# The 3x3 convolution of a two-layer kernel rewritten as minimal filtering F(2,3) along the width

## What is computed

```
xn  = groupnorm(x)                                   # 32 groups of 16 channels
f   = relu(Wc @ xn + bc)                             # 512 -> 128 channels
dyn = relu(Wck . stack(gate_kernel, band_maxima) + bck)   # per image: a 3x3 kernel, 128 x 128 channels
y   = conv3x3(f, dyn) + b_ad                         # 128 -> 128 channels
x1  = x + Wf @ y + bf                                # 128 -> 512 channels
out = x1 + grouped_conv3x3(groupnorm(x1), K)         # 32 groups, 16 -> 16 channels
```

## Time and profile before

| | us |
|---|---|
| median of 3 runs | 3616.2 (3615.72 to 3616.76) |
| the profiled execution's own time | 3616.31 |
| its span from first to last instruction | 3614.6 |
| PE busy | 3498.8 (97%) |
| DVE busy | 2532.3 (70%) |
| ACT busy | 2109.9 (58%) |
| POOL busy | 965.3 (27%) |

### The profile page before, as it was taken

How to read it: one execution, slowest core, us unless ns; L and a number is a source line. 1 busy time by engine, 2 the same in 40 slices (tenths; PEclk the granted TensorE clock), 3 DMA queues, 4 the chain that set the end, 5 groups by cost and what they waited for, 6 DMA issues and landing times.

```text
span 3614.6 us, 60228 instructions
## 1 busy us (share of the span) xinstructions
PE 3498.8 (97%) x18688; PEld 2789.1 (77%) x18688; DVE 2532.3 (70%) x5365; ACT 2109.9 (58%) x3559; POOL 965.3 (27%) x1039
## 2 busy tenths in 40 slices
PE   5799999999999999999999999999999999999996
PEld 4677877777877778877778777778777778777785
DVE  7676777776767677777667777767777777776742
ACT  4365555665555665655655556655556655556654
POOL 2033222232222232222332222322222322223323
PEclk9899999999999999999999999999999999999998
DMA  5467767677767667767677667677676777676666
GB/s 122 142 193 190 190 178 185 200 195 192 185 180 195 191 184 193 190 183 197 189 188 190 186 178 207 197 190 186 178 191 194 188 195 186 182 199 187 170 156 158
DMA packets 317577, 666.88 MB, mean 184 GB/s; under 512 B 58863, under 2 KB 288242, under 8 KB 288645
## 3 DMA queue, kind: packets, MB, share of 16 engines
q1 hardware_dynamic: 317317, 663.34, 68.5%
HBM read 355.00 MB, written 308.28 MB: 184 GB/s over the span
## 4 chain that ended last, share of the span: by engine, by line
PE 90%; issue 5%; DVE 4%; DMA 1%; POOL 0%; DVEq 0%; ACT 0%; SPq 0%; POOLq 0%; ACTq 0%
PE pb L853 15%; PE pb L855 15%; PE pb L854 15%; PE pac L853 7%; PE pd L853 7%; PE pd L855 7%; PE pd L854 7%; PE pac L854 6%; PE pac L855 6%; PE pac L925 2%; PE pac L862 1%; DVE x1b L764 1%; PE ps L918 1%; DMA big<-x 0%; DVE va L596 0%
## 5 line engine op out<-in xcount | busy, mean ns | idle before, releaser
L407 POOL TENSOR_TENSOR hl<-un,hl 128x384 f16<-128x384 f32 x1024 | 937.6, 916 | 2570.2 <-ACT hl L432 2566.6
L432 ACT ACTIVATE hl<-un 128x384 f16<-128x384 f32 x1024 | 539.0, 526 | 427.8 <-PE pb L855 361.7
L428 ACT ACTIVATE un<-big,b_t,s_t 128x384 f32<-128x384 f32 x1024 | 709.7, 693 | 16.1 <-DMA big<-x_rows 16.1
L853 PE MATMUL pb<-fh,dynh 128*128 128x480 f32 (+1 forms) x1440 | 548.2, 381 | 0.0
L855 PE MATMUL pb<-fh,dynl 128*128 128x480 f32 (+1 forms) x1440 | 545.3, 379 | 0.0
L854 PE MATMUL pb<-fl,dynh 128*128 128x480 f32 (+1 forms) x1440 | 544.4, 378 | 0.0
L774 DVE SCALAR_TENSOR_TENSOR big<-pd,kout,big 96x768 f32<-96x768 f32 x256 | 258.8, 1011 | 382.6 <-PE pd L855 382.6
L853 PE MATMUL pd<-hl,k_h 128*96 128x384 f16 x1536 | 507.0, 330 | 18.8 <-POOL hl L407 18.8
L774 DVE SCALAR_TENSOR_TENSOR big<-pb,kout,big 96x768 f32<-96x768 f32 x256 | 258.9, 1011 | 351.8 <-PE pb L855 351.8
L853 PE MATMUL pb<-hl,k_h 128*96 128x384 f16 x1536 | 504.9, 329 | 0.0
L854 PE MATMUL pd<-hl,k_h 128*96 128x384 f16 x1536 | 504.8, 329 | 0.0
(11 more groups left out here) (115 smaller groups left out, 5241.6 us busy)
## 6 DMA issues: line engine op xcount, KB each, us to landing
big<-x SPq DMA_DIRECT2D x128, 1152.0 KB, 9.8
x_rows<-x1b SPq DMA_DIRECT2D x128, 1152.0 KB, 5.6
big<-x_rows SPq DMA_DIRECT2D x128, 1152.0 KB, 12.7
out<-big SPq DMA_DIRECT2D x128, 1152.0 KB, 6.2
big<-x_rows SPq DMA_DIRECT2D x256, 192.0 KB, 13.2
x_rows<-mrow SPq DMA_DIRECT2D x64, 96.0 KB, 1.9
big<-kt SPq DMA_DIRECT2D x4, 288.0 KB, 9.7
big<-kt SPq DMA_DIRECT2D x2, 192.0 KB, 11.0
```

Source lines behind the costliest of these rows:

```text
L407: pool.tensor_tensor(hl[:, g % HL_RING, 1, :, 1:W + 1], un[:, g % U_RING], hl[:, g % HL_RING, 0, :, 1:W + 1], ALU.subtract).then_inc(hl_lo, 1)
L428: act.activation(un[:, g % U_RING], t_slot(g // GQ)[:, g % GQ], ACT.Identity, bias=b_t[:, g:g + 1], scale=s_t[:, g:g + 1]).then_inc(u_done, 1)
L432: act.activation(hl[:, g % HL_RING, 0, :, 1:W + 1], un[:, g % U_RING], ACT.Copy).then_inc(hl_hi, 1)
L853: pe.matmul(acc, high_w, high_x, start=start, stop=False)
```

## The change

F(2,3) computes two neighbouring output columns of a row of a 3-tap filter with four products in place of six. From f, four planes are made ("frequencies" in the code): with columns f0..f3 of a pair these are f2 - f0 and f3 - f1 (one instruction for both), f2 + f1, and f2 - f1. The filter gets four combinations of its three taps per row: the two outer taps as they are, and (outer sum + middle) and (outer sum - middle). Four products are added over the three rows, and the two outputs are combined from them.

What is new, by engine:

- PE: the B stage has 3 tiles of 16 rows x 24 column pairs = 384 columns, 4 frequencies x 3 rows x 3 matmuls: 108 matmuls, 24 of them 360 columns wide at the image's edge. It uses 7 PSUM banks in turn.
- POOL: `v_sums` makes the four planes in three instructions a tile behind one that zeroes the border columns; `v_low` the low part of tiles 0 and 1; `y_low` that of two of the three output tiles; `dyn_sums` the tap combinations.
- ACT: `f_relu` writes f without splitting it, `v_high` the high part of the four planes (960 or 768 elements a partition), `m2_out` one product out of PSUM, `y_high` on 768 elements; `dyn_relu` and `dyn_high` take the place of one instruction.
- DVE: no `f_low`; `v_low` for tiles 2 to 4, `y_sums` and `y_rest` (four instructions of 384 elements a tile), one `y_low`. `dyn_low` moves to the start of a step. Moments and maxima of chunks 2, 3 and 0 stand in the C and D stage, those of chunk 1 alone in B.
- SP: the weights `wc` and `dyn_rows` are loaded anew for each image behind the B stage, since their place in SBUF is shared with a plane. x1's chunk and the squares also lie in planes.

The diff's core:

```diff
-EARLY = {3: (0, 1), 4: (2, 3)}
+EARLY = {1: (0, 1), 2: (2, 3)}
+WROWS = 16
+NW = H // WROWS
+WM = W // 2
+WN = WROWS * WM
+FREQ = 4
+FREQ_ORDER = (2, 3, 0, 1)
+B_BANK = [0, 1, 2, 3, 4, 5, 6, 0, 2, 3, 4, 5]
+PER_B = NW * FREQ
+POOL_TILES = 2
+POOL_Y = 2
...
-STATS_IN_B = (1, 2, 3)
...
-MOMENTS_AT = {3: (0, 0), 4: (0, 1)}
-MAXIMA_AT = {5: 0}
+GATES_AFTER = 29
+MOMENTS_AT = {0: (2, 0), 1: (2, 1), 2: (3, 0), 3: (3, 1), 4: (0, 0), 5: (0, 1)}
+MAXIMA_AT = {7: 2, 9: 3, 10: 0}
...
-KERNEL_INPUTS_AFTER = 11
-KERNELS_AFTER = 12
+CENTRED_AT = 11
+KERNEL_INPUTS_AFTER = 12
+KERNELS_AFTER = 13
...
+            def v_sums(n, t):
+                nr = TILES[t][1]
+                f, v = f_tile(t), v_tile(vl_sums, t)
+                if t == 0:
+                    reached(pool, sq_done, n * Q)
+                some = ones[:, 0:2 * nr].rearrange("p (r two) -> p r two", two=2)
+                pool.tensor_tensor(f[:, :, 0:W + 2:W + 1], some, some, ALU.subtract).then_inc(pad_done, 1)
+                pool.wait_ge(pad_done, n * NT + t + 1)
+                pool.wait_ge(f_done, n * NT + t + 1)
+                if t == 0:
+                    pool.wait_ge(dyn_done, n + 1)
+                pool.tensor_tensor(v[:, :, 0:2, :].rearrange("p r k m -> p r m k"), f[:, :, 2:W + 2].rearrange("p r (m k) -> p r m k", k=2),
+                                   f[:, :, 0:W].rearrange("p r (m k) -> p r m k", k=2), ALU.subtract)
+                even, odd = (f[:, :, 1 + i:1 + i + W - 1:2] for i in range(2))
+                pool.tensor_tensor(v[:, :, 2, :], odd, even, ALU.add)
+                pool.tensor_tensor(v[:, :, 3, :], odd, even, ALU.subtract).then_inc(v_done, 1)
...
+            def v_low(n, t):
+                pool.wait_ge(v_hi, n * NT + t + 1)
+                pool.tensor_tensor(v_tile(vl, t), v_tile(vl_sums, t), f32(v_tile(vh, t)), ALU.subtract).then_inc(v_lo_pool, 1)
...
+                for t in range(NT):
+                    v_sums(n, t)
+                    if 1 <= t <= POOL_TILES:
+                        v_low(n, t - 1)
+                for t in range(POOL_Y):
+                    y_low(n, t)
+                    if d:
+                        d_groups(n - 1, EARLY[t + 1])
                 if d:
-                    d_groups(n - 1, range(G))
-
+                    d_groups(n - 1, range(EARLY_GROUPS, G))
+                else:
+                    kernels_low()
+                if more:
+                    dyn_sums(n + 1)
...
-                act.activation(fh[:, r0 + 1:r0 + 1 + nr, 1:W + 1], pac[:, t % 2, 0:nr * W].rearrange("p (r w) -> p r w", w=W),
-                               ACT.Relu).then_inc(f_hi, 1)
+                if t == 0:
+                    reached(act, sq_done, n * Q)
+                if t == NT - 1:
+                    reached(act, hl_lo, (n - 1) * G)
+                elif t >= 2:
+                    act.wait_ge(v_done, n * NT + t - 1)
+                act.activation(f_tile(t)[:, :, 1:W + 1], pac[:, t % 2, 0:nr * W].rearrange("p (r w) -> p r w", w=W),
+                               ACT.Relu).then_inc(f_done, 1)
...
+            def v_high(n, t):
+                act.wait_ge(v_done, n * NT + t + 1)
+                if t == 0:
+                    reached(act, x1_out[Q - 1], n * 16)
+                act.activation(v_tile(vh, t), v_tile(vl_sums, t), ACT.Copy).then_inc(v_hi, 1)
...
+            def m2_out(n, t):
+                act.wait_ge(b_mm, n * PER_B + t * FREQ + 2)
+                act.activation(y_columns(t, 1), b_bank(t * FREQ + 1), ACT.Identity, bias=badc[:, 0:1],
+                               scale=0.5).then_inc(m2_done, 1)
...
+            def dyn_relu(n):
+                act.wait_ge(dyn_mm, n + 1)
+                act.activation(dynl_sums[:, :, 0:2, :], dyn_acc[:, :, 0:2 * CM].rearrange("p d (k m) -> p d k m", k=2), ACT.Relu)
+                act.activation(middle, dyn_acc[:, :, 2 * CM:3 * CM], ACT.Relu).then_inc(dyn_f, 1)
+
             def dyn_high(n):
-                act.wait_ge(dyn_mm, n + 1)
-                act.activation(dynh_banks, dyn_acc, ACT.Relu).then_inc(dyn_hi, 1)
+                act.wait_ge(dyn_g, n + 1)
+                act.activation(dynh[:, :, :, :], dynl_sums[:, :, :, :], ACT.Copy).then_inc(dyn_hi, 1)
...
-                        f_high(n, t - 1)
-                f_high(n, NT - 1)
-                for t in range(NT):
-                    if t in EARLY and d:
+                        f_relu(n, t - 1)
+                    if 2 <= t < NT:
+                        v_high(n, t - 2)
+                f_relu(n, NT - 1)
+                if d:
+                    root_second(n - 1)
+                v_high(n, NT - 2)
+                m2_out(n, 0)
+                v_high(n, NT - 1)
+                if not d:
+                    kernels(0)
+                y_high(n, 0)
+                for t in range(1, NW):
+                    if d:
                         d_groups(n - 1, EARLY[t])
+                    m2_out(n, t)
+                    if not d:
+                        kernels(t)
                     y_high(n, t)
...
+                if more:
+                    dyn_relu(n + 1)
                 square(n, Q - 1)
+                if more:
+                    dyn_high(n + 1)
...
+            def v_low(n, t):
+                vec.wait_ge(v_hi, n * NT + t + 1)
+                vec.tensor_tensor(v_tile(vl, t), v_tile(vl_sums, t), f32(v_tile(vh, t)), ALU.subtract).then_inc(v_lo_dve, 1)
...
+            def y_sums(n, t):
+
+                vec.wait_ge(m2_done, n * NW + t + 1)
+                vec.scalar_tensor_tensor(out=y_columns(t, 0), in0=b_bank(t * FREQ), scalar=0.5, in1=y_columns(t, 1),
+                                         op0=ALU.mult, op1=ALU.add)
+                vec.scalar_tensor_tensor(out=y_columns(t, 1), in0=b_bank(t * FREQ), scalar=0.5, in1=y_columns(t, 1),
+                                         op0=ALU.mult, op1=ALU.subtract).then_inc(eo_done, 1)
+
+            def y_rest(n, t):
+
+                vec.wait_ge(eo_done, n * NW + t + 1)
+                vec.wait_ge(b_mm, n * PER_B + t * FREQ + 3)
+                vec.scalar_tensor_tensor(out=y_columns(t, 0), in0=b_bank(t * FREQ + 2), scalar=-1.0, in1=y_columns(t, 0),
+                                         op0=ALU.mult, op1=ALU.add)
+                vec.wait_ge(b_mm, n * PER_B + t * FREQ + 4)
+                vec.scalar_tensor_tensor(out=y_columns(t, 1), in0=b_bank(t * FREQ + 3), scalar=badc[:, 1:2], in1=y_columns(t, 1),
+                                         op0=ALU.add, op1=ALU.add).then_inc(y_done, 1)
...
-                for t in range(NT):
-                    for i in range(t * Q, (t + 1) * Q):
-                        if i >= AHEAD:
-                            x_low(n, odd, i)
-                    if t:
-                        f_low(n, t - 1)
-                f_low(n, NT - 1)
+                if d:
+                    x1_mean_rows(n - 1)
+                dyn_low(n)
+                for i in range(AHEAD, UNITS):
+                    x_low(n, odd, i)
                 if d:
                     x1_group_means(n - 1)
                     x1_variances(n - 1)
-                y_low(n, 0)
-                for t in range(1, NT):
-                    if t == SCALES_BEFORE and d:
-                        for i in range(SCALE_STEPS):
-                            x1_scales(n - 1, i)
-                    if more and t <= len(STATS_IN_B):
-                        moments(n + 1, 1 - odd, STATS_IN_B[t - 1])
-                        maxima(n + 1, 1 - odd, STATS_IN_B[t - 1])
-                    y_low(n, t)
+                v_low(n, 2)
+                v_low(n, 3)
+                y_sums(n, 0)
+                if d:
+                    for i in range(SCALE_STEPS):
+                        x1_scales(n - 1, i)
+                v_low(n, 4)
+                y_rest(n, 0)
+                if more:
+                    moments(n + 1, 1 - odd, 1)
+                y_sums(n, 1)
+                y_rest(n, 1)
+                if more:
+                    maxima(n + 1, 1 - odd, 1)
+                y_sums(n, 2)
+                y_rest(n, 2)
+                y_low(n, 2)
...
+                r0 = t * WROWS
+                if t == 0:
+                    pe.wait_ge(v_lo_pool, POOL_TILES * (n + 1))
+                else:
+                    pe.wait_ge(v_lo_dve, (NT - POOL_TILES) * n + t + 1)
+                for j, k in enumerate(FREQ_ORDER):
+                    i = t * FREQ + j
+                    if i == 2:
+                        pe.wait_ge(f_done, (n + 1) * NT)
+                    if i == 7 or i == 10:
+                        pe.wait_ge(eo_done, n * NW + (1 if i == 7 else 2))
+                    if i == 8:
+                        pe.wait_ge(y_done, n * NW + 1)
+                    acc = b_bank(i).rearrange("p (r m) -> p r m", m=WM)
+                    for dy in (1, 0, 2):
+                        lo, hi = max(r0 + dy - 1, 0), min(r0 + dy - 1 + WROWS, H)
+                        at = lo - (r0 + dy - 1)
```

(16 more changed lines are left out.)

229 lines of the change are left out of this document (132 added, 97 removed).

## The result

The changed kernel takes **3874.2 us** (median of 4 runs, 3873.1 to 3880.3) beside 3616.1 for the kernel before: ratio 1.072, 95% interval 1.0707 to 1.0733. It is slower by 258 us. First its page, engines and the chain that ended last; in the earlier trace rows PE had 90% of the chain.

A forecast was written before the change was run, and what follows sets the result against it. PE was taken as the bound, busy nearly all of a 109.5 us step. Terms -9.9 + 9.5 + 2.9 + 2.3 + 0.5 + 3.0 gave +8.3 a step, hence 3875 us; its own range 3770 to 4020, stated range 3650 to 4010.

The forecast's parts named there:

- Products of B: B stage: 108 matmuls starting 0.184 us apart take 19.6 us in place of 29.46, -9.9 us a step.
- A, +9.5: A stage: late start, POOL and DVE taking turns, and last matmuls make 23.4 us against 13.9, +9.5 a step.
- fixed sum of turns, whoever goes first: In A, B cannot start before DVE's 15 x_low (7.7) and POOL's sums and v_low (11.4) are through, 19.1 us.
- Point (2): Sign in A: x_low mean over 1.2 us, POOL busy nearly throughout, PE waiting for xs, A 21 to 27 us.
- Root, +2.9: In B, the second tile waits for v_low 3, behind v_high 3 and root_second on ACT: +2.9 us a step, bounds 2.4 to 3.5.
- point (3): Sign in B: PE waits some 3 us for vl by DVE once behind each x1_spread.
- Way into C: C's first unit waits for the last tile's y_low, with layer 1 groups late: +2.3 us a step, bounds 0.5 to 3.5.
- Pair 8: C and D: maxima at pair 7 make the first residual behind pair 8 late, so PE waits +0.5 us.
- pair 11, +3.0: C and D: DVE's maxima and prep work after output 9 make PE wait +3.0 us more for unit 18's bank.
- point (6): Sign for PE throughout: the granted clock stays at 1.00.
- The rival: PE's clock falls in A and at B's start, 2.6 us for each of 32 steps, about 3960 us; chance 0.13.
- The third rival: A's feeding keeps PE's pace, A grows under 1.2 us, step -1.2, about 3575 us and faster; chance 0.12.

The follow-up runs named there:

- the run with one SBUF input: Changed kernel with x_low of units 5 to 19 (from image 1 on) taking its first input from PSUM instead of x, its value then wrong: 3684.1 us.
- The same kind of POOL work without consumers: The kernel before, with POOL given 36 subtractions of constant SBUF tensors in A, needed only by ACT's first layer 1 group, which waits for their end: 3701.3 us.
- the run with copies: The kernel before with nine pieces of unneeded POOL work in A, three of each piece's four instructions being one-input copies, the small first a subtraction: 3616.3 us, ratio 1.0005.

## Why the prediction was right, and where it was so by luck

Predicted 3875, measured 3874.2; 8.3 a step predicted, 8.5 measured in the mean of two steps (8.35 over 30). The terms:

- *Products of B, -9.9.* 18.8 us once nothing waits in it, hence -10.7: 0.8 off. The pace is 0.174, not 0.184. The old kernel's last tile did run at 0.182 in all its 27 matmuls of 384 columns (from the row below to D's first at 1174.23 in the earlier trace rows), so the reading was right; why the planes' matmuls are a little faster is not shown by any run.

```profile
1169.32 0.34 PE L853 MATMUL pb<-fh,dynh 128*128 128x384 f32 x1
```

- *A, +9.5.* Measured +9.0 and +8.1, mean +8.6 (+8.5 over 30 steps). The late start (3.8) is 3.56. From the start of unit 5 to the end of the last `x_low` pass 18.65 us in the first step and 17.76 in the next, where the prediction has a "fixed sum of turns, whoever goes first" of 19.1; POOL has no pause from its first sum to its second `v_low` in either. So the sum held nearly, though strict turns did not: DVE goes four or seven `x_low` ahead, and POOL catches up while DVE waits. That the order matters little is borne out by the two patterns, 22.9 and 22.0, and by the run with `v_high` later, which changed who is waited for and left A at 22.3. POOL's prices fit as well: 1.08, 0.59 and 2.26 us for 480, 240 and 960 elements (medians in the run with one SBUF input), said 1.07, 0.61 and 2.0. The 1.40 of a turn is in no row; the earlier trace rows bound it by 1.2 (2.41 / 2) and 1.46 (1234.95 to 1237.87 for two), so the 15 `x_low` could have been put at 4.7 to 8.6 and not only 7.7. Point (2) gave `x_low` a mean over 1.2 us; it was 1.08 over the run, 0.64 and then 1.31 in A of the first step. The sign of being wrong, "`x_low` keeps 0.65 beside POOL", came true for the first four to seven of them and yet the sum stood. That two SBUF inputs beside POOL are the cause is shown by the run with one (6.2 us of A). The same kind of POOL work without consumers cost only 2.7: nothing made A wait for its end there, so that 12.5 us of POOL fell into A in place of 18.7. How much of A's length is turns and how much is the waiting for POOL's results is not separated by that.
- *Root, +2.9.* 2.67 of B, shown by moving it. PE waits 2.46 for DVE's `v_low` 3 once a step, as point (3) has it.
- *Way into C, +2.3.* 2.53, and 0.97 where B holds a slow stretch; 1.8 in the mean over 30 steps. The groups of layer 1 in ACT's order were named as what is late; moving `m2_out` ahead of them took 1.2 of it.
- *Pair 8, +0.5; pair 11, +3.0.* 0.45 and 3.32, of which 0.55 at pair 11 was there before (at 1223.00 in its trace): +0.45 and +2.8.
- *The clock, 0.* This step of the prediction failed, point (6). Of the two steps read above C and D hold 3.0 and 1.4 us that no wait explains, at a granted clock of 0.50 behind the waits into C and at pair 11: +2.2. Over 30 steps it is 2.1 in C and D and 0.7 in B, and the 0.7 is given back by the shorter wait into C. The rival had the mechanism and, by chance, the price (2.6), but placed it in A and at B's start. In A it cost nothing, since DVE was late there anyway, and at B's start it did not come.

8.6 - 10.7 + 2.7 + 2.5 + 0.45 + 2.8 + 2.2 = 8.55. The sum agrees to 0.3 because the missed clock, +2.2, stands against products that are 0.8 and an A that is 0.9 cheaper than said. That is luck: without it the sum would have been off by about 2 us a step, 60 us in all.

The third rival, "A hides everything", fell: A never grew by less than 8 in a kernel that computes the whole. But its sign was reached by another way than the prediction had: with A as long as ever, taking away the waits of B, C and D was enough. The prediction had booked +8.7 for these as if the change forced them. They were the price of an order of instructions, and what the change itself costs is A's 8 to 9 against B's 10.7.

By the Trainium skill (SBUF — State Buffer, Who interferes with whom) a DVE instruction with at most one SBUF input, outside the modes that use two ports, does not contend with GpSimd, and one with two contends with a GpSimd instruction that reads SBUF, over a pair of ports that is locked by one of them at a time. The run with one SBUF input agrees (5.02 to 1.08). The Trainium skill (the same section) lets the order of issue decide who blocks, and does not say for how many instructions: here DVE kept it for four or for seven in a row, and in the run with copies for whole runs of four.

Open: why DVE yields to POOL after each instruction in the late half of A, but only after four or seven in its first half, and not at all in the run with copies. Open too: which of several waits of 2.3 to 3.3 us is followed by a slow stretch; in the changed kernel the steps differ in it, and mostly alternate. The 8 us of A were not taken away in any kernel that computes the whole; a version in which POOL's sums run with fewer SBUF reads beside `x_low` wasn't tried.

## What to carry to other kernels

A saving on the bound engine is worth its size only if the chains that feed it get shorter by as much. List each border of stages, with the engine whose *order* decides it, and ask what stands in front of the needed instruction there; here four such places turned a stage shorter by 10.7 us into a step longer by 8.5, and three of them were mended by moving a call or two each. Two fixes are not worth their sum: each idle time on DVE can be spent once. The waits of PE of 2.3 to 3.3 us cost here up to about 1.5 us above their length where a slow stretch of 3 us followed; taking them away paid, filling them did not.

## What the runs showed of the hardware that was not expected

- One two-input POOL instruction (480 columns, 1.08 us alone) stood for 5.02 us beside `x_low` at 0.64 each, in 13 of 30 steps; in 16 it stood for 3.2. So a run of short instructions on DVE can shut POOL out until it ends or for some of its length.
- POOL copies never slowed DVE (739 against 733 ns) although they themselves stretched from 0.35 to 2.83 us. A two-input subtraction of 16 columns in the same run stretched from 0.22 to 2.58.
- TensorE's granted clock fell to 0.50 for about 3 us behind waits of 2.3 (the root moved) to 3.3 us, although it had been busy for 12 us and more ahead of those into C and at pair 11. Behind a wait of 1.30 in front of C it stayed at 1.00; in A it fell also where PE waited 1.08 and then 1.69 us, with ends 3.6 us apart (to 1101.92 and to 1105.49). Filling the wait into C with 20 matmuls moved the fall to pair 11 and brought 4 us of 3874; filling those in A with 61 kept A at 1.00 and brought nothing (3887.7 us).
